# Memory cross-attention of a two-layer decoder: softmax sums from TensorE, the division on the output, and fp16 half products for query and gate

## The chip, the cores and the metric

The kernel runs on one core of one Trainium2 chip. The metric is the device time of one execution in microseconds (us); smaller is better.

## The reference

Input x is 8 batches of 256 tokens by 256 channels, float32. Six layers follow each other, each as x = x + layer(layernorm(x)): attention with 16 heads of 128, a linear attention over a context of 64 tokens, a feed-forward layer with 4-bit weights, an attention over channels, the memory layer, and a feed-forward layer with ternary weights. The change is in the memory layer; cut to what matters it is

```python
x = rmsnorm(hidden_states, norm_w)
q = (x @ wq.T).reshape(B, L, NH, HD)          # NH = 16 heads of HD = 16
k = (memory_tokens @ wk.T).reshape(B, M, NH, HD)   # M = 64
v = (memory_tokens @ wv.T).reshape(B, M, NH, HD)
attn = jnp.einsum('blhd,bmhd->bhlm', q, k) * scale
attn = jnp.where(memory_mask[:, None, None, :], attn, -jnp.inf)
attn = jax.nn.softmax(attn, axis=-1)
attn = jnp.nan_to_num(attn, nan=0.0)
out = jnp.einsum('bhlm,bmhd->blhd', attn, v).reshape(B, L, C)
out = out @ wo.T
gate = jax.nn.sigmoid(x @ wg.T)
return gate * out
```

## The kernel before

The program has two parts. `attention_part` (to 558 us of the span) computes the first attention in 64 steps, 16 heads by 4 pairs of batches, and beside it prepares the weights of later layers at numbered steps: `KV_HI` is step 59, `LAST` is 63. Its scores, exponentials, column sums and products with the rows of X are staged over three steps, so that step i works on step i-1 and i-2 too.

`streams_part` runs the other five layers. A batch is a stream; four streams share the chip at a time, and batches 4 to 7 follow batches 0 to 3 in the same buffers, so there are two rounds, 558 to 735 us and 735 to 912 us. A stream has two PSUM banks, `PA` and `PB`. Each layer of a stream is a list of stages with an engine and a length each (`work`). `turns_by_engine` lays the stages of all streams out in time by these lengths and so fixes the order of each engine's queue; at run time every engine goes through its queue in that order and waits for semaphores. The lengths decide the order only.

A layer starts with its norm: `stats` (L1556), `aggr` (L1562), `eps` (L1568 for the memory layer, L1571 for the others) on VectorE, the power on GpSimd (L1416), the normalised rows, four transposes by TensorE (L1746) and their copy to SBUF by ScalarE. In the memory layer this copy (L1455) also multiplies by `norm_w`. Then TensorE makes queries (`mem_q`, L1731) and gate (`mem_g`, L1738) in float32, four products of 128x128 by 256 columns each. Every tile t of 128 tokens then goes through

- `s`: mask and scores of 16 heads by 64 keys into both banks (PE, L1855 and L1860)
- `max`, `sub` (DVE, L1681, L1684), `exp` (ACT, L1506), `sum`, `rd` (DVE, L1688, L1691: sums of the exponentials of each head, and their reciprocals), `pn` (POOL, L1427: 1024 exponentials times the 16 reciprocals)
- `pt` (PE, L1868: eight transposes), `pte` (ACT, L1510), `o` (PE, L1875: eight products with a 32-column stationary, two heads each, that go to four different groups of 32 output rows in turn), `ote` (ACT, L1516: copy to `ot` times `any_key`)

The tile 1 scores wait for tile 0's `ote`, because they use the same banks. `mem_out` (PE, L1738), `mem_go` and `mem_add` (DVE, L1666, L1670) end the layer. In the ternary layer, `m0`, `c0`, `c1` (L1701 to L1710) make two scalars per row. `pair_matmuls` (L75 to L77) multiplies two float32 operands that are split into fp16 halves, as three fp16 products.

```python
for j in range(XH // 2):
    rows = slice(j % 4 * 2 * XD, (j % 4 + 1) * 2 * XD)
    last = nc.tensor.matmul(PA[s][rows, j // 4 * P:(j // 4 + 1) * P],
                            g.v1[:, s, j].rearrange("p a e -> p (a e)"), pt[s][:, j * P:(j + 1) * P],
                            start=True, stop=True)
```

## Time and profile before

| | before |
|---|---|
| median of 3 runs | 916.41 us (916.15 to 917.59) |
| the profiled execution | 914.14 us, span 912.3 us |
| mean granted TensorE clock | 0.994 |
| TensorE busy | 848.8 us (93%) |
| VectorE busy | 707.6 us (78%) |
| ScalarE busy | 539.0 us (59%) |
| GpSimd busy | 373.0 us (41%) |

The span is the time from the first to the last instruction in the profile; 1.8 us of the execution lie around it. A float32 product shows as two records of TensorE, an fp16 one as one. The length of a record is that of one product in a pipeline, so the cost of a series is read from start to start.

### The profile page before, as it was taken

To read this page: it belongs to the slowest core of one execution; us is meant where nothing else is said; L and a number is where in the kernel's file an instruction comes from. 1 tells how busy PE (TensorE), PEld (TensorE's weight loads), DVE (VectorE), ACT (ScalarE), POOL (GpSimd) and SP (SyncE) were. 2 spreads that over 40 slices of the span, in tenths; PEclk is the share of its full clock that TensorE was granted. 3 is DMA by queue.
4 is the path that set the end of the run, shared out by engine and by line. 5 is a ranking of instruction groups with operands and counts; after the bars stand their busy time and mean duration, and the time that the engine had idled before them with its cause. 6 is when DMAs were issued, how large, how long until landed. Compare 5 with 4: busy or idle time off the path is not lost. (4 is left out here: it accounts for less than half of the span.)

```text
span 912.3 us, 18715 instructions
## 1 busy us (share of the span) xinstructions
PE 848.8 (93%) x6868; PEld 630.7 (69%) x6868; DVE 707.6 (78%) x1749; ACT 539.0 (59%) x1285; POOL 373.0 (41%) x358
## 2 busy tenths in 40 slices
PE   6888998999999999999999998999978889999786
PEld 3555766777777777777777776887855578777554
DVE  5647967887788788877887774997688779886985
ACT  1655576665666566656665655464566864546676
POOL 6014555545555555545554644052242031522410
PEclk9999999999999999999999999999999999999999
DMA  9133131101110111011100000000000010000001
GB/s 279 40 83 93 22 94 36 31 6 35 35 26 8 35 35 35 0 35 35 35 0 11 1 1 2 2 1 1 1 1 1 1 47 1 1 1 1 1 1 47
DMA packets 34723, 25.56 MB, mean 28 GB/s; under 512 B 9492, under 2 KB 31596, under 8 KB 34668
## 3 DMA queue, kind: packets, MB, share of 16 engines
q1 hardware_dynamic: 34380, 24.56, 10.1%
q8 instruction: 35, 0.57, 0.3%
q10 hardware_dynamic: 288, 0.26, 0.1%
q14 instruction: 20, 0.16, 0.1%
HBM read 22.65 MB, written 2.17 MB: 27 GB/s over the span
## 5 line engine op out<-in xcount | busy, mean ns | idle before, releaser
L502 POOL CAST exp_hi<-exp_scores 128x1024 f16<-128x1024 f32 x64 | 67.0, 1047 | 199.4 <-ACT exp_scores L628 199.4
L504 POOL TENSOR_TENSOR exp_lo<-exp_scores,exp_hi 128x1024 f16<-128x1024 f32 x64 | 140.7, 2198 | 5.1
L628 ACT ACTIVATE exp_scores<-banks,exp_bias,unscale 128x256 f32<-128x256 f32 x256 | 141.0, 560 | 2.1
L75 PE MATMUL banks<-value_out_hi,xn_t_hi 128*128 128x256 f16 x512 | 139.6, 273 | 0.8 <-DVE X L961 0.5
L76 PE MATMUL banks<-value_out_lo,xn_t_hi 128*128 128x256 f16 x512 | 139.5, 273 | 0.0
L77 PE MATMUL banks<-value_out_hi,xn_t_lo 128*128 128x256 f16 x512 | 139.5, 273 | 0.0
L1119 PE MATMUL banks<-qk 128*128 128x256 f32 x512 | 121.6, 380 | 8.5 <-ACT exp_scores L628 8.4
L1119 PEld LDWEIGHTS banks<-qk 128*128 128x128 f32 x512 | 96.6, 190 | 29.4 <-issue 8.7
L961 DVE SCALAR_TENSOR_TENSOR X<-banks,colsum,X 128x256 f32<-128x256 f32 x256 | 106.2, 478 | 12.8 <-DVE colsum L952 11.4
L573 ACT ACTIVATE qk<-banks 128x512 f32<-128x512 f32 x128 | 75.8, 601 | 58.9 <-PE banks L77 58.9
L75 PE MATMUL banks<-xn_t_hi,head_weights_hi 128*128 128x512 f16 x256 | 96.9, 378 | 2.4 <-ACT qk L573 1.6
L933 DVE TENSOR_REDUCE neg_rowmax<-banks 128x4 f32<-128x1024 f32 x64 | 78.2, 1222 | 26.7 <-PE banks L1119 26.6
L77 PE MATMUL banks<-xn_t_hi,head_weights_lo 128*128 128x512 f16 x256 | 97.0, 379 | 0.0
L76 PE MATMUL banks<-xn_t_lo,head_weights_hi 128*128 128x512 f16 x256 | 96.9, 379 | 0.0
L1416 POOL TENSOR_TENSOR rstd_stream<-rstd_stream,neg_half 128x2 f32<-128x2 f32 x36 | 26.0, 724 | 137.4 <-DVE rstd_stream L1571 127.2
L624 ACT ACTIVATE exp_bias<-neg_rowmax,unscale 128x4 f32<-128x4 f32 x64 | 18.8, 293 | 99.8 <-DVE neg_rowmax L933 99.8
L76 PEld LDWEIGHTS banks<-value_out_lo,xn_t_hi 128*128 128x128 f16 x512 | 50.1, 98 | 11.8
L442 POOL TENSOR_TENSOR head_weights_lo<-head_weights,head_weights_hi 128x512 f16<-128x512 f32 x32 | 38.8, 1213 | 47.5 <-ACT head_weights_hi L526 47.4
L75 PEld LDWEIGHTS banks<-value_out_hi,xn_t_hi 128*128 128x128 f16 x512 | 50.1, 98 | 10.0 <-DVE X L961 3.4
L1427 POOL TENSOR_TENSOR big_stream<-big_stream,den_stream 128x1024 f32<-128x1024 f32 x16 | 30.3, 1901 | 60.9 <-DVE den_stream L1691 60.9
L77 PEld LDWEIGHTS banks<-value_out_hi,xn_t_lo 128*128 128x128 f16 x512 | 50.1, 98 | 5.8
L628 ACT ACTIVATION_READ_ACCUMULATOR exp_scores<-banks,exp_bias,unscale 128x1 f32 x256 | 50.8, 198 | 0.0
(254 smaller groups left out, 1962.4 us busy)
## 6 DMA issues: line engine op xcount, KB each, us to landing
head_weights<-in_wqkv_d SPq DMA_DIRECT2D x32, 128.0 KB, 3.8
weight_absmax_rows<-across_partitions SPq DMA_DIRECT2D x15, 256.0 KB, 4.2
X<-in_x_d SPq DMA_DIRECT2D x4, 512.0 KB, 7.6
head_weights<-in_wqkvt_d SPq DMA_DIRECT2D x16, 128.0 KB, 3.5
head_weights<-in_w_o_d SPq DMA_DIRECT2D x16, 128.0 KB, 3.5
out<-X SPq DMA_DIRECT2D x8, 256.0 KB, 2.1
ternary_then_kv_and_rows<-in_c_fc_d SPq DMA_DIRECT2D x1, 1024.0 KB, 5.0
ternary_then_kv_and_rows<-in_c_proj_d SPq DMA_DIRECT2D x1, 1024.0 KB, 8.0
```

The lines of the kernel that those rows point to most:

```text
L75: nc.tensor.matmul(out, lhs[0], rhs[0], start=first, stop=False)
L76: nc.tensor.matmul(out, lhs[0], rhs[1], start=False, stop=False)
L77: return nc.tensor.matmul(out, lhs[1], rhs[0], start=False, stop=last)
L442: nc.gpsimd.tensor_tensor(wlo[:, u, 2 * a:2 * a + 2], wst[:, u, 2 * a:2 * a + 2], whi[:, u, 2 * a:2 * a + 2], ALU.subtract).then_inc(wlo_r ...
L502: nc.gpsimd.tensor_copy(probh[:, s1_.par], prob[:, s1_.par]).then_inc(exph_ready, 1)
L504: nc.gpsimd.tensor_tensor(probl[:, s1_.par], prob[:, s1_.par], probh[:, s1_.par], ALU.subtract).then_inc(expl_ready, 1)
L573: nc.scalar.activation(qk[:, par, s, :], qk_ps[s], ACT.Copy).then_inc(qk_ready, 1)
L628: last = nc.scalar.activation(prob[:, s1_.par, t, :], sc_ps[t // ST][:, t % ST, :], ACT.Exp, bias=nbias[:, t:t + 1], scale=unscale[:, s1_. ...
L933: nc.vector.tensor_reduce(nmax[:, :], sc_both, AX.X, ALU.max, negate=True).then_inc(nmax_ready, 1)
L961: last = nc.vector.scalar_tensor_tensor(out=g.X[:, TP * s2.p + t, :], in0=xm_ps[t // ST][:, t % ST, :], scalar=csum[:, t:t + 1], in1=g.X[: ...
L1119: last = nc.tensor.matmul(sc_ps[b][:, t, :], qk[:, par, 0, q], qk[:, par, 1, kk], start=True, stop=True)
L1427: nc.gpsimd.tensor_tensor(by_head(s), by_head(s), den[s][:, t, :].unsqueeze(2).broadcast_to([P, XH, M]), ALU.mult).then_inc(mem_pn[t], 1)
```

## The change

In the attention part, the weights of query and gate are prepared once: multiplied by `norm_w` and their absolute maxima taken (step 59), the maxima spread over the partitions by two DMAs on the SP queue, behind the last head's, and scaled (step 61), and split into fp16 halves (step 62: ScalarE the high, VectorE the low one). GpSimd sets a tile `own_ones`: for each of a pair of heads ones in its 64 rows and 16 columns.

In the memory layer, the transposed rows are split into halves (ScalarE copies the high half, VectorE subtracts for the low one: a new `lo`), and query and gate become 12 fp16 products each. `sum`, `rd`, `pn` and `ote` are gone: the transposes take the exponentials as they are. `o` gets a second product for each pair of heads, with `own_ones`, that leaves the sum of each head in the 16 rows of its output. `rs` takes the reciprocal of these 128x256 sums from PSUM into `xt`, `on` multiplies output, `any_key` and reciprocal into `ot`; both are on VectorE.

In all layers of the streams `eps` moves from VectorE to GpSimd, and in the ternary layer `c1` is folded into `m0` and `c0`. The planner's lengths follow (`rs` .42, `on` .42, `o` 1.16). The two buffers of rows for maxima move into `nf4_part0` and `nf4_part1`.

```diff
+        sp.wait_ge(mem_max_ready, 2)
+        sp.dma_start(spread(6, P, 2), mem_max[:, :]).then_inc(mem_max_out, 16)
+        sp.wait_ge(mem_max_out, 16)
+        sp.dma_start(mem_rows.rearrange("p q s -> p (q s)"), gathered(6, P, 2)).then_inc(mem_max_in, 16)
...
+        nc.gpsimd.memset(g.own_ones[:, :, :], 0.0).then_inc(own_ones_set, 1)
+        for a in range(2):
+            pool.wait_ge(own_ones_set, a + 1)
+            nc.gpsimd.memset(g.own_ones[a * M:(a + 1) * M, a, :], 1.0).then_inc(own_ones_set, 1)
+        pool.wait_ge(own_ones_set, 3)
...
+            if known(i) and i == KV_HI + 3:
+                act.wait_ge(mem_step, 5)
+                for n, (w, (hi, _)) in enumerate(zip(mem_weights, mem_parts)):
+                    nc.scalar.activation(hi, w, ACT.Copy, scale=mem_scale[:, n:n + 1]).then_inc(mem_hi_ready, 1)
...
+            if i == KV_HI:
+
+                dve.wait_ge(late_loads, 16 * len(g.small_loads))
+                for w in (g.wq1, g.wg1):
+                    for k in range(KT):
+                        nc.vector.tensor_scalar(w[:, k, :], w[:, k, :], g.normw[:, k:k + 1], None,
+                                                ALU.mult).then_inc(mem_normed, 1)
+                for n, w in enumerate(mem_weights):
+                    dve.wait_ge(mem_normed, KT * (n + 1))
+                    nc.vector.tensor_reduce(mem_max[:, n:n + 1], w, AX.X, ALU.max,
+                                            apply_absolute_value=True).then_inc(mem_max_ready, 1)
...
+            if i == KV_HI + 2:
+                dve.wait_ge(mem_max_in, 16)
+                nc.vector.tensor_reduce(mem_all[:, :], mem_rows.rearrange("p q s -> p s q"), AX.X,
+                                        ALU.max).then_inc(mem_step, 1)
...
+            if i == KV_HI + 3:
+                dve.wait_ge(mem_hi_ready, 2)
+                for n, (w, (hi, lo)) in enumerate(zip(mem_weights, mem_parts)):
+                    nc.vector.scalar_tensor_tensor(out=lo, in0=w, scalar=mem_scale[:, n:n + 1], in1=hi, op0=ALU.mult,
+                                                   op1=ALU.subtract)
...
-        return [f"{layer}_stats DVE .66 {after}", f"{layer}_aggr DVE .16", f"{layer}_eps DVE .08", f"{layer}_pow POOL .67",
+        return [f"{layer}_stats DVE .66 {after}", f"{layer}_aggr DVE .24", f"{layer}_eps POOL .2", f"{layer}_pow POOL .67",
...
-    work += norm_work("mem", "fat_add", ["xt ACT .74"])
-    work += ["mem_q PE 1.8", "mem_kbd DVE .67 fat_add", "mem_g PE 1.74 mem_xt", "mem_qt ACT .49 mem_q", "mem_ge ACT .49 mem_g"]
+    work += norm_work("mem", "fat_add", ["xt ACT .49", "lo DVE .6"])
+    work += ["mem_q PE 1.36", "mem_kbd DVE .67 fat_add", "mem_g PE 1.36 mem_lo", "mem_qt ACT .49 mem_q", "mem_ge ACT .49 mem_g"]
     for t in range(ST):
         work += [f"mem{t}_{w}" for w in ("s PE 1.19" + (" mem_qt mem_kbd mem_ge" if t == 0 else ""),
-                                         "max DVE 1.13", "sub DVE 1.14", "exp ACT .96", "sum DVE 1.13", "rd DVE .17",
-                                         "pn POOL 1.86", "pt PE 1.02", "pte ACT .92", "o PE .58", "ote ACT .36")]
+                                         "max DVE 1.13", "sub DVE 1.14", "exp ACT .96", "pt PE 1.02", "pte ACT .92",
+                                         "o PE 1.16", "rs DVE .42", "on DVE .42")]
...
+            if part == "eps":
+                ln = norms[layer]
+                pool.wait_ge(ln["mv"], nth_norm(layer, s))
+                inside, eps = (1.0 + 1e-6, LN_EPS * 1e-6) if layer == "mem" else (1.0, LN_EPS)
+                nc.gpsimd.tensor_scalar(rstd[s][:, :], mv[s][:, :, 1], inside, eps, ALU.mult, ALU.add).then_inc(ln["veps"], 1)
...
-            elif part == "pn":
-                t = tile_of(layer)
-                pool.wait_ge(mem_rden[t], n[s])
-                nc.gpsimd.tensor_tensor(by_head(s), by_head(s), den[s][:, t, :].unsqueeze(2).broadcast_to([P, XH, M]),
-                                        ALU.mult).then_inc(mem_pn[t], 1)
...
-                elif layer == "mem":
-                    for k in range(KT):
-                        last = nc.scalar.activation(xt[s][:, k, :], tiles(PA[s])[:, k, :], ACT.Copy,
-                                                    scale=g.normw[:, k:k + 1])
-                    last.then_inc(mem["xt_ready"], 1)
                 else:
-                    nc.scalar.activation(xh[s], tiles(PA[s]), ACT.Copy).then_inc(ffn_hi if layer == "ffn" else ter_hi, 1)
+                    nc.scalar.activation(xh[s], tiles(PA[s]), ACT.Copy).then_inc(xt_hi[layer], 1)
...
-                nc.scalar.activation(qt[s][:, :, :], tiles(PB[s]), ACT.Copy).then_inc(mem_q, 1)
+                nc.scalar.activation(qt[s][:, :, :], tiles(PB[s]), ACT.Copy, scale=g.mem_unscale[:, 0:1]).then_inc(mem_q, 1)
             elif name == "mem_ge":
                 act.wait_ge(mem_g_full, n[s])
-                nc.scalar.activation(gate[s][:, :, :], tiles(PA[s]), ACT.Tanh, scale=0.5).then_inc(mem_g, 1)
+                nc.scalar.activation(gate[s][:, :, :], tiles(PA[s]), ACT.Tanh, scale=g.mem_half_unscale[:, :]).then_inc(mem_g, 1)
...
-            elif layer in ("mem0", "mem1") and part == "ote":
-
-                t = tile_of(layer)
-                act.wait_ge(mem_o_full[t], n[s])
-                nc.scalar.activation(ot[s][:, :, t * P:(t + 1) * P], PA[s][:, 0:KT * P].rearrange("p (k n) -> p k n", k=KT),
-                                     ACT.Copy, scale=g.anykey[:, s:s + 1]).then_inc(mem_o[t], 1)
...
-            elif part == "lo" and layer in ("ffn", "ter"):
-                dve.wait_ge(ffn_hi if layer == "ffn" else ter_hi, n[s])
+            elif part == "lo":
+                dve.wait_ge(xt_hi[layer], n[s])
...
-            elif part == "sum":
-                dve.wait_ge(mem_exp[t], n[s])
-                nc.vector.tensor_reduce(den[s][:, t, :], by_head(s), AX.X, ALU.add).then_inc(mem_sum[t], 1)
-            elif part == "rd":
-                dve.wait_ge(mem_sum[t], n[s])
-                nc.vector.reciprocal(den[s][:, t, :], den[s][:, t, :]).then_inc(mem_rden[t], 1)
+            elif part == "rs":
+                dve.wait_ge(mem_o_full[t], n[s])
+                nc.vector.reciprocal(xt[s][:, t, :], PA[s][:, KT * P:2 * KT * P]).then_inc(mem_rden[t], 1)
+            elif part == "on":
+                dve.wait_ge(mem_rden[t], n[s])
+                by_tile = lambda ap: ap.rearrange("p (k n) -> p k n", k=KT)
+                nc.vector.scalar_tensor_tensor(out=ot[s][:, :, t * P:(t + 1) * P], in0=by_tile(PA[s][:, 0:KT * P]),
+                                               scalar=g.anykey[:, s:s + 1], in1=by_tile(xt[s][:, t, :]), op0=ALU.mult,
+                                               op1=ALU.mult).then_inc(mem_o[t], 1)
...
-                nc.vector.tensor_scalar(small[s][:, 5:6], small[s][:, 4:5], g.tscale[:, 0:1], float(np.sqrt(1e-5)),
-                                        ALU.mult, ALU.max).then_inc(ter_step[s], 1)
+                nc.vector.tensor_scalar(small[s][:, 5:6], small[s][:, 4:5], g.tscale_root[:, 0:1],
+                                        float(np.sqrt(1e-5 / 255.0)), ALU.mult, ALU.max).then_inc(ter_step[s], 1)
             elif part == "c0":
-                dve.wait_ge(ter_step[s], s // STREAMS * 3 * ST + 3 * t + 1)
-                nc.vector.reciprocal(small[s][:, 6:7], small[s][:, 5:6]).then_inc(ter_step[s], 1)
+                dve.wait_ge(ter_step[s], s // STREAMS * 2 * ST + 2 * t + 1)
+                nc.vector.reciprocal(small[s][:, 7:8], small[s][:, 5:6]).then_inc(ter_scale[t], 1)
                 nc.vector.tensor_scalar(small[s][:, 9 + t:10 + t], small[s][:, 5:6], small[s][:, 5:6],
-                                        g.tscale255[:, 0:1], ALU.mult, ALU.mult).then_inc(ter_step[s], 1)
-            elif part == "c1":
-                dve.wait_ge(ter_step[s], s // STREAMS * 3 * ST + 3 * t + 2)
-                nc.vector.tensor_scalar(small[s][:, 7:8], small[s][:, 6:7], float(np.sqrt(255.0)), None,
-                                        ALU.mult).then_inc(ter_scale[t], 1)
...
-                features_first(PB[s], g.wq1, xt[s]).then_inc(mem_q_full, 1)
+                for m in range(KT):
+                    for k in range(KT):
+                        last = pair_matmuls(nc, tiles(PB[s])[:, m, :],
+                                            [w[:, k, m * P:(m + 1) * P] for w in g.mem_halves[0]],
+                                            [x[:, k, :] for x in (xh[s], xl[s])], k == 0, k == KT - 1)
+                last.then_inc(mem_q_full, 1)
             elif name == "mem_g":
-                tokens_first(PA[s], xt[s], g.wg1).then_inc(mem_g_full, 1)
+                for t in range(ST):
+                    for k in range(KT):
+                        last = pair_matmuls(nc, tiles(PA[s])[:, t, :],
+                                            [x[:, k, t * P:(t + 1) * P] for x in (xh[s], xl[s])],
+                                            [w[:, k, :] for w in g.mem_halves[1]], k == 0, k == KT - 1)
+                last.then_inc(mem_g_full, 1)
...
-                pe.wait_ge(mem_pn[t], n[s])
+                pe.wait_ge(mem_exp[t], n[s])
...
-                    last = nc.tensor.matmul(PA[s][rows, j // 4 * P:(j // 4 + 1) * P],
-                                            g.v1[:, s, j].rearrange("p a e -> p (a e)"), pt[s][:, j * P:(j + 1) * P],
-                                            start=True, stop=True)
+                    for at, values in ((j // 4, g.v1[:, s, j]), (KT + j // 4, g.own_ones[:, :, :])):
+                        last = nc.tensor.matmul(PA[s][rows, at * P:(at + 1) * P], values.rearrange("p a e -> p (a e)"),
+                                                pt[s][:, j * P:(j + 1) * P], start=True, stop=True)
...
```

The planner's order changes in the memory layer. TensorE, round one: the products that stand ahead of the first scores. Numbers behind names are the streams; L1818 is the channel attention's first product of stream 3, L1731 and L1738 with `wq1` and `wg1` are query and gate, L1855 and L1860 the scores. Before:

```order
L1818 MATMUL banks<-xn_stream_3 128x256 x4
L1731 MATMUL banks<-xt_stream_0,wq1 128x256 x4
L1738 MATMUL banks<-wg1,xt_stream_0 128x256 x4
L1746 MATMUL banks<-ident,xn_stream_1 128x128 x4
L1826 MATMUL banks<-ident,big_stream_3 128x128 x4
L1746 MATMUL banks<-ident,xn_stream_2 128x128 x4
L1855 MATMUL banks<-mask_bias,ones 128x512 x2
L1860 MATMUL banks<-big_stream_0,qt_stream_0 128x256 x4
```

After the change (the query of stream 0, a turn, the gate of stream 0, two turns, the query of stream 1 and the channel attention's last product of stream 3 stand ahead of these rows; L75 to L77 are half products, L1893 and L1898 the scores):

```order
L75 MATMUL banks<-mem_w1_hi,xt_stream_1 128x256
L76 MATMUL banks<-mem_w1_lo,xt_stream_1 128x256
L77 MATMUL banks<-mem_w1_hi,xt_stream_1 128x256
L1893 MATMUL banks<-mask_bias,ones 128x512 x2
L1898 MATMUL banks<-big_stream_0,qt_stream_0 128x256 x4
L75 MATMUL banks<-xt_stream_2,mem_w0_hi 128x256
L76 MATMUL banks<-xt_stream_2,mem_w0_hi 128x256
L77 MATMUL banks<-xt_stream_2,mem_w0_lo 128x256
L75 MATMUL banks<-xt_stream_2,mem_w0_hi 128x256
```

The first scores of stream 0 have moved behind query and gate of stream 1.

VectorE, round one, inside the layer (before: L1681 max, L1684 sub, L1688 sum, L1691 rd):

```order
L1684 TENSOR_TENSOR big_stream_3<-banks,den_stream_3 128x1024
L1681 TENSOR_REDUCE den_stream_0<-banks 128x16
L1688 TENSOR_REDUCE den_stream_3<-big_stream_3 128x16
L1684 TENSOR_TENSOR big_stream_0<-banks,den_stream_0 128x1024
L1691 RECIPROCAL den_stream_3<-den_stream_3 128x16
L1681 TENSOR_REDUCE den_stream_1<-banks 128x16
L1688 TENSOR_REDUCE den_stream_0<-big_stream_0 128x16
L1684 TENSOR_TENSOR big_stream_1<-banks,den_stream_1 128x1024
L1681 TENSOR_REDUCE den_stream_2<-banks 128x16
```

After (L1710 max, L1713 sub, L1717 rs, L1721 on):

```order
L1710 TENSOR_REDUCE den_stream_3<-banks 128x16
L1717 RECIPROCAL xt_stream_0<-banks 128x256
L1713 TENSOR_TENSOR big_stream_3<-banks,den_stream_3 128x1024
L1721 SCALAR_TENSOR_TENSOR ot_stream_0<-banks,any_key,xt_stream_0 128x2x128
L1717 RECIPROCAL xt_stream_1<-banks 128x256
L1721 SCALAR_TENSOR_TENSOR ot_stream_1<-banks,any_key,xt_stream_1 128x2x128
L1717 RECIPROCAL xt_stream_2<-banks 128x256
L1721 SCALAR_TENSOR_TENSOR ot_stream_2<-banks,any_key,xt_stream_2 128x2x128
L1710 TENSOR_REDUCE den_stream_0<-banks 128x16
L1713 TENSOR_TENSOR big_stream_0<-banks,den_stream_0 128x1024
```

Where sum and reciprocal of a tile stood between maxima, there is now a reciprocal of 256 elements a row and the multiplication, later in the stream's tile, and the second tiles' maxima come behind three of them.

## Rows read from the trace of the kernel before

**Rows 1.** Windows of the first round: start:end, length, then busy us (instructions) per engine.

```profile
596.50:643.10 46.60, 46.35 (x342) 37.23 (x341) 38.91 (x111) 25.00 (x69) 19.68 (x30) 1.00 0.01 1
643.10:649.10 6.00, 6.00 (x40) 4.96 (x39) 2.42 (x10) 4.98 (x13) 0.70 (x1) 1.00 0.00 0
649.10:659.10 10.00, 10.00 (x51) 8.28 (x52) 6.11 (x13) 4.46 (x8) 2.56 (x2) 1.00 0.00 1
659.10:684.30 25.20, 20.62 (x192) 14.89 (x196) 21.73 (x25) 14.80 (x19) 9.93 (x6) 0.93 0.01 1
684.30:700.10 15.80, 14.69 (x134) 11.37 (x127) 13.76 (x32) 8.95 (x14) 5.43 (x5) 1.00 0.01 2
700.10:734.80 34.70, 27.20 (x203) 16.90 (x201) 27.73 (x83) 28.01 (x31) 3.78 (x5) 1.00 0.07 23
```

**Rows 2.** Timeline of TensorE, first round: start us, length us, group xrecords.

```profile
641.22 1.89 PE L1818 MATMUL banks<-xn_stream 128*128 128x256 f32 x8
642.94 1.89 PE L1731 MATMUL banks<-xt_stream,wq 128*128 128x256 f32 x8
...
648.03 1.03 PE L1860 MATMUL banks<-big_stream,qt_stream 64*128 64x256 f32 x8
648.99 1.99 PE L1738 MATMUL banks<-big_stream,xt_stream 128*128 128x256 f32 x8
...
667.13 0.65 PE L1875 MATMUL banks<-mid_stream,v 128*32 128x128 f32 x16 [0.58 <-ACT mid_stream L1510]
667.71 1.09 PE L1868 MATMUL banks<-ident,big_stream 128*128 128x128 f32 x8
```

**Rows 3.** Timeline of VectorE: first row maximum and last gated addition of round one.

```profile
649.11 1.23 DVE L1681 TENSOR_REDUCE den_stream<-banks 128x16 f32<-128x1024 f32 x1 [2.62 <-PE banks L1860]
...
699.36 0.69 DVE L1670 SCALAR_TENSOR_TENSOR X<-gate_stream,X 128x512 f32<-128x512 f32 x1
```

**Rows 4.** Groups by line and shape, VectorE reciprocals: xcount | busy us, mean ns.

```profile
L1691 DVE RECIPROCAL den_stream<-den_stream 128x16 f32<-128x16 f32 x16 | 3.6, 237 | 0.0
...
L1609 DVE RECIPROCAL den_stream<-den_stream 128x32 f32<-128x32 f32 x8 | 2.8, 351 | 0.1
...
L793 DVE RECIPROCAL nf_divide<-nf_s_by_column 128x66 f32<-128x66 bf16 x1 | 0.6, 567 | 0.1
```

**Rows 5.** Groups by line and shape, other VectorE and ScalarE work of the layers.

```profile
L1688 DVE TENSOR_REDUCE den_stream<-big_stream 128x16 f32<-128x1024 f32 x16 | 19.4, 1212 | 1.9 <-ACT big_stream L1506 1.9
...
L1585 DVE TENSOR_TENSOR xt_stream<-banks,xt_stream 128x512 f16<-128x512 f32 x16 | 10.9, 678 | 0.0
...
L1571 DVE TENSOR_SCALAR rstd_stream<-mv_stream 128x2 f32<-128x2 f32 x28 | 7.7, 273 | 0.4
...
L1516 ACT ACTIVATE ot_stream<-banks,any_key 128x256 f32<-128x256 f32 x16 | 7.5, 468 | 7.1 <-PE banks L1875 7.1
...
L1613 DVE SCALAR_TENSOR_TENSOR xn_stream<-banks,lin_scale,den_stream 128x256 f32<-128x256 f32 x16 | 7.0, 478 | 0.2
```

**Rows 6.** Timeline of VectorE inside the memory layer.

```profile
671.18 1.21 DVE L1688 TENSOR_REDUCE den_stream<-big_stream 128x16 f32<-128x1024 f32 x1
672.31 1.22 DVE L1684 TENSOR_TENSOR big_stream<-banks,den_stream 128x1024 f32<-128x1024 f32 x1
```

**Rows 7.** Groups by line and shape, GpSimd.

```profile
L1427 POOL TENSOR_TENSOR big_stream<-big_stream,den_stream 128x1024 f32<-128x1024 f32 x16 | 30.3, 1901 | 60.9 <-DVE den_stream L1691 60.9
...
L507 POOL TENSOR_TENSOR rowsum_inverse_halves<-rowsum_inverse,rowsum_inverse_halves 128x4 f16<-128x4 f32 x64 | 13.7, 215 | 6.5 <-DVE rowsum_inverse_halves L918 6.5
```

**Rows 8.** The chain of waits, first round: four transposes, then 16 fp16 products.

```profile
595.26 0.44 PE banks L1746 x4
595.69 1.75 PE banks L1800 x16
```

**Rows 9.** Timeline of VectorE at the end of the attention part.

```profile
514.30 1.22 DVE L933 TENSOR_REDUCE neg_rowmax<-banks 128x4 f32<-128x1024 f32 x1 [1.96 <-PE banks L1119]
...
541.13 0.22 DVE L949 TENSOR_SCALAR colsum_raw<-banks,unscale 128x4 f32<-128x4 f32 x1 [0.48 <-PE banks L1199]
```

More of the change, by code:

```diff
@@ L2040, in decoder @@
     g.normw = table("normw", KT)
+    g.mem_halves = [[sb(f"mem_w{n}_{half}", [P, KT, D], F16) for half in ("hi", "lo")] for n in range(2)]
+    g.mem_unscale = sb("mem_w_unscale", [P, 2])
+    g.mem_half_unscale = sb("mem_w_half_unscale", [P, 1])
     g.headmask = table("headmask", XH // KT)
```

62 lines of the change are left out of this document (36 added, 26 removed).

## Prediction

> **What bounds the kernel now.** I read the windows of the first round first, since the streams run twice with the same order and almost the same length. In the feed-forward and channel attention stretch TensorE is busy 46.35 of 46.60 us, and it stays full while the memory layer starts, 643.1 to 659.1 us; VectorE is busy there 2.42 of 6 and 6.11 of 10 us. Then it turns over: from 659.1 to 700.1 us VectorE is busy 35.5 of 41.0 us and TensorE waits 5.7 us. In the ternary stretch no engine is full; TensorE, VectorE and ScalarE are each near 80% [rows 1]. So the change is worth something in two places with two different limits: what it takes off TensorE's queue before the first scores, and what it puts on or takes off VectorE between the first row maximum at 649.1 and the last gated addition at 700.05 us (699.36 + 0.69), a stretch of 51.0 us [rows 3].
>
> **Query and gate.** A float32 product of one kind takes from the start of the series at 641.22 to the next at 642.94, 1.73 us for four products [rows 2]. Sixteen fp16 products of the same 256 columns take 1.75 us, 0.109 each [rows 8], so twelve take 1.31: 0.42 saved, for each of two products of a stream, 3.4 us of TensorE a round. But the order changes as well. Before, query, gate, three sets of four transposes and the scores stand between the end of the last channel product, 643.1, and the first scores' end, 649.1. In the new order query and gate of stream 1 and the last channel product stand there too: four series at 1.31, three sets of transposes at 0.44 [rows 8], one float32 series at 1.92 (start 648.99, seen from its end) and the scores with mask at 1.2, 9.7 us; I add 0.3 for `lo`, which the query now waits for. VectorE has room for it. The first scores end 4.0 us later than before, and what was done in that time needn't be done afterwards.
>
> **The stretch from there.** VectorE is busy 6.11 + 21.73 + 13.76 = 41.6 us in the 51.0 [rows 1]. Eight tiles have a maximum, a subtraction and a sum each, at 1.13 from start to start [rows 6] for a length of 1.21 [rows 5]: lengths overlap by 0.08. With eight small reciprocals at 0.237 - 0.08 = 0.16 [rows 4] these are 28.4 us; 13.2 us are other work.
>
> - Gone: `sum` and `rd`, 8 x (1.13 + 0.16) = 10.3 us.
> - New: `on`, 8 x 0.40 by the like multiplication of 128x256 from PSUM, 0.478 long [rows 5], 3.2 us.
> - New: `rs`. No row shows a reciprocal of 256 elements. 16, 32 and 66 elements take 237, 351 and 567 ns [rows 4]: 7.1 and 6.4 ns for each further one, where the multiplication of 256 takes 478 in all. The lower bound is that 478 ns, if the slope came from something else than the operation; the upper is 0.351 + 224 x 0.0071 = 1.94 us. I take the slope of the widest row: 0.567 + 190 x 0.0064 = 1.78, less the overlap 1.70, 8 x 1.70 = 13.6 us. The order that the planner made counts on 0.42.
> - The other work: the last channel addition, its statistics and means fall before the new first scores (1.6 us less), four `eps` go to GpSimd (4 x 0.273, 1.1 less) [rows 5], the last stream's `lo` comes in (0.6 more, L1585's 0.678 less the overlap) [rows 5]: 11.1 us.
>
> The maxima and subtractions stay, 18.1. Sum 18.1 + 13.6 + 3.2 + 11.1 = 46.0 us. VectorE waits at two places: the second maximum is behind query and gate of stream 2 and the scores (1.4 us), the fourth behind those of stream 3 (1.2). That makes 48.6 for 51.0. With the later start: +4.0 - 2.4 = **+1.6 us a round**.
>
> The Trainium skill, VectorE: DVE Perf Modes (First, the fixed hardware budget), says that a reciprocal is an iterative divide with a repeat count of 8. At the clock that its Specifications give, 0.96 GHz, my estimate from that page is 8.3 ns an element and 2.1 us for 256; `rs` would add 3 us a round to the sum above. The rows, at 6.4 to 7.1 ns, have the same kind of cost but a smaller one, and the sum goes by them.
>
> **`o` doubled.** Eight products and their 16 records show 0.65 us [rows 2]. The bounds for sixteen: 0.65, if the second of a pair fits in the shadow of the first, and 2.0, if it doesn't overlap at all with a product before it on the same output rows: a float32 product of 256 columns is 0.43 (1.73 / 4), of 128 columns 0.22, eight pairs that follow at that pace make 1.73 and the last result 0.28. I take 1.2, twice the row. TensorE then has about 42.6 us of work in the 48.6: 45.3 before [rows 1], 5.4 that moved ahead, 1.7 off the later queries and gates, 4.4 more in `o`. So it is hidden behind VectorE, as long as it stays near 1.2.
>
> **The chain of a tile.** `sum`, `rd`, `pn` (1.90 us on GpSimd [rows 7]) and `ote` (0.47 on ScalarE [rows 5]) were 3.7 us from exponential to transposes and from output to the next scores; `rs` and `on` are 2.1. That helps only where VectorE waits, and it is in the two waits that I left.
>
> **Rest of a round.** Eight `c1` at 0.07 and the `eps` of the other layers in full VectorE stretches at 0.08 are worth 1.2 us. The `eps` on GpSimd costs 0.2 (by L507, 0.215 [rows 7]) against less on VectorE, and a norm's rows wait for it a few times: 0.5 back. **-0.7 us a round.** ScalarE's lighter load is worth nothing: it was waiting.
>
> **Attention part.** Step 59 puts four multiplications and two maxima, about 2.5 us, where VectorE is idle 1.96 us before the next row maximum [rows 9]; TensorE doesn't wait for that maximum yet. The two DMAs have a step and a half, on a queue with nothing behind them but the end. Step 61's 1.5 us fit in idle time. Step 62 adds two subtractions, 1.3 us, just before the first statistics, where VectorE's next wait is only 0.48 us [rows 9]: I take 0.7 for all (0 to 2). The memsets of `own_ones` are under 0.5 us on an idle GpSimd, zero; without that cover the first weights' halves, and the first scores behind them, would be that much later.
>
> **Sum:** 2 x (1.6 - 0.7) + 0.7 = +2.5 us on the span of 912.3 in an execution of 914.14. That execution lies 2.3 us under the median of the runs, 916.41, and I add the difference to the median: **918.9 us**. About 0.2% (1.8 us) is what a measurement tells from no change, so this is just beyond it.
>
> **Rivals.**
> - *Pairs on the same output rows wait for each other.* Before, neighbours in `o` go to different groups of rows, which is how eight products fit in 0.65 us; now each second one follows its own pair. `o` is then 2.0, TensorE's work in the stretch 49.0 us, above VectorE's 46.0, and the first `rs` starts 0.8 later. I price it at +2 us a round: 922.9. For it: the pace of one after another, 1.73, is far above the 0.65 seen. The Trainium skill, TensorEngine Tiling (Array Packing), Key Properties, says that different tiles work in parallel; no trace here has two products in a row on the same one. Chance 0.24.
> - *The reciprocal runs like other operations at this width* (faster side). The rows stop at 66 elements. At 0.48 instead of 1.78, `rs` takes 10.4 us a round off VectorE, and TensorE's 42.6 us plus a wait bound the stretch: -5 a round, 908.9. It decides from about 1.2 us down; at 1.5 the change is nil. Against it: three widths on one line. Chance 0.12.
> - *Waits vanish more than I count* (the shorter tile chain, and VectorE's `eps` that had stood still for GpSimd, 0.273 against 0.16 for an undisturbed one): -3 a round, 912.9. Chance 0.14.
> - *The order fits lengths that aren't true.* `rs` is planned at a quarter of its length, so maxima queue behind reciprocals whose sums aren't there, and ScalarE and TensorE wait in turn: +3 a round, 924.9. Chance 0.14.
> - That the change doesn't do what it says I leave out: the order shows every stage in its new place.
>
> **How the numbers follow.** The forecast has 0.36. Its own spread of some 3 us puts a quarter of it within 0.2%, and a little below. The range from 911 to 925 leaves out most of the fast reciprocal and half of the misfit, under 0.2. Faster by over 0.2% (under 914.6): 0.12, most of 0.14 and a little of the forecast, 0.26. Within: 0.22, from the forecast and the edges of its neighbours. Slower: 0.52.
>
> **What would show it.** The first row maximum some 4 us later in the round, the gated additions ending 1 to 2 us later; `rs` at 1.7 to 1.8 us, and VectorE the releaser of TensorE's waits in the layer; `o` at 1.2 us from start to start; query and gate at 1.3 each; no `pn` on GpSimd; 0 to 2 us more before the streams start. A `rs` under 1.2 us, or VectorE idle over 5 us in the layer while TensorE is full, would prove the forecast wrong.

## The result, and the profile after

The changed kernel takes **924.85 us** (median of 5 runs, 923.42 to 927.95), the kernel before 916.41: 1.0092 times as long, 95% interval 1.0069 to 1.0116. The forecast was 918.9. The profiled execution has a span of 923.1 us against 912.3, and that of before lay 2.3 us under its own median, so the traces show 10.8 us where the medians show 8.4.

The groups that answer to [rows 4, 5, 7, 8], by line and shape (the last two columns: busy us with mean ns, and idle time before with its releasers):

```profile
L1717 DVE RECIPROCAL xt_stream<-banks 128x256 f32<-128x256 f32 x16 | 28.0, 1747 | 0.0
...
L1614 DVE TENSOR_TENSOR xt_stream<-banks,xt_stream 128x512 f16<-128x512 f32 x24 | 16.4, 682 | 2.9 <-ACT xt_stream L1503 2.8
...
L75 PE MATMUL banks<-xt_stream,mem_w_hi 128*128 128x256 f16 x32 | 8.8, 274 | 0.2
...
L1466 POOL TENSOR_SCALAR rstd_stream<-mv_stream 128x2 f32<-128x2 f32 x36 | 7.8, 216 | 219.3 <-DVE mv_stream L1600 219.0
...
L1721 DVE SCALAR_TENSOR_TENSOR ot_stream<-banks,any_key,xt_stream 128x256 f32<-128x256 f32 x16 | 7.7, 479 | 0.3
```

The new operations last what the prediction said: `rs` 1.75 us (1.78), `on` 0.48, `eps` on GpSimd 0.216. The doubled `o`, on TensorE's timeline (start, length, group xrecords):

```profile
672.04 0.45 PE L1914 MATMUL banks<-mid_stream,v 128*32 128x128 f32 x8
672.28 0.42 PE L1914 MATMUL banks<-mid_stream,own_ones 128*32 128x128 f32 x8
672.50 0.44 PE L1914 MATMUL banks<-mid_stream,v 128*32 128x128 f32 x8
672.72 0.44 PE L1914 MATMUL banks<-mid_stream,own_ones 128*32 128x128 f32 x8
673.09 1.09 PE L1906 MATMUL banks<-ident,big_stream 128*128 128x128 f32 x8
```

Sixteen products in 1.05 us, start to next start. No pair waits for its neighbour on the same output rows.

**Where the time went.** Marks of the two timelines, each piece in us (the pieces tile the span). The next-to-last scores are the 63rd of the attention part's 64; the first stream operation is VectorE's on `headmask`; fat_e is the channel attention's first product, and its last in a round is that of the fourth stream:

| piece | before | after | difference |
|---|---|---|---|
| start to the next-to-last scores | 536.21 | 537.01 | +0.8 |
| from there to the first stream operation | 21.95 | 27.73 | **+5.8** |
| round one: to the last fat_e | 83.06 | 84.29 | +1.2 |
| to the first row maximum | 7.89 | 11.68 | **+3.8** |
| to the fourth gated addition | 50.25 | 47.87 | -2.4 |
| round two: to the last fat_e | 118.54 | 117.62 | -0.9 |
| to the first row maximum | 7.90 | 11.68 | **+3.8** |
| to the fourth gated addition | 48.75 | 47.66 | -1.1 |
| to the end | 37.75 | 37.56 | -0.2 |

The streams together cost 4.2 us, the attention part 5.8, the start 0.8. The fences below mark rows left out between two shown by `...`. The two ends of the big piece in the attention part, on VectorE's and then TensorE's timeline of the changed kernel (in brackets: idle time before, and its releaser):

```profile
537.82 2.71 DVE L1045 SCALAR_TENSOR_TENSOR mem_w_lo<-wq,mem_w_scale,mem_w_hi 128x512 f16<-128x512 f32 x1 [0.99 <-ACT mem_w_hi L662]
540.45 0.74 DVE L1045 SCALAR_TENSOR_TENSOR mem_w_lo<-wg,mem_w_scale,mem_w_hi 128x512 f16<-128x512 f32 x1
...
543.16 1.22 DVE L954 TENSOR_REDUCE neg_rowmax<-banks 128x4 f32<-128x1024 f32 x1
```

```profile
537.01 1.89 PE L1169 MATMUL banks<-qk 128*128 128x256 f32 x8
...
547.18 3.46 PE L1169 MATMUL banks<-qk 128*128 128x256 f32 x8 [3.99 <-ACT exp_scores L645]
```

The same places in the kernel before, the row maximum and the two sets of scores:

```profile
538.13 1.22 DVE L933 TENSOR_REDUCE neg_rowmax<-banks 128x4 f32<-128x1024 f32 x1
```

```profile
536.21 1.89 PE L1119 MATMUL banks<-qk 128*128 128x256 f32 x8
...
542.16 1.97 PE L1119 MATMUL banks<-qk 128*128 128x256 f32 x8
```

VectorE waits 0.99 us for ScalarE's high halves, then needs 2.71 us for one subtraction that takes 0.74 the second time. GpSimd's timeline has the reason beside it, the subtraction that makes the exponentials' low half (exp_lo):

```profile
537.85 2.13 POOL L521 TENSOR_TENSOR exp_lo<-exp_scores,exp_hi 128x1024 f16<-128x1024 f32 x1
```

The long subtraction ends at 540.53, 0.55 us after exp_lo's end at 539.98: it stood still until GpSimd was through. The Trainium skill, GPSIMD Engine Reference (1. Specifications), lists GpSimd's way to SBUF as shared with VectorE, with contention where VectorE has two SBUF inputs, as here. The row maximum behind it comes at 543.16 (538.13 before), the exponentials after it, and TensorE stands for 3.99 us. The granted clock around it:

```profile
540.00:550.00 10.00, 5.84 (x49) 4.58 (x48) 7.85 (x26) 3.89 (x11) 3.93 (x4) 0.84 0.01 2
550.00:560.00 10.00, 9.14 (x93) 7.61 (x92) 8.38 (x22) 4.98 (x13) 4.95 (x6) 0.99 0.00 0
...
564.70:574.70 10.00, 9.96 (x36) 7.58 (x38) 2.55 (x3) 3.44 (x7) 4.93 (x4) 0.70 0.01 2
```

These are windows: bounds, length, busy us of TensorE, its weight loads, VectorE, ScalarE and GpSimd, and the granted clock. In a window with a mean of 0.84 or 0.70, part of the time is at 1.2 GHz and the rest at 2.4. After the 3.99 us of standing, the scores at 547.18 take 3.46 us for what took 1.97. The last window is the beginning of the streams, where TensorE has stood 3.16 us. In the kernel before it had stood 3.10 us, and their first 10 us have a clock of 0.85:

```profile
558.20:568.20 10.00, 10.00 (x44) 7.54 (x45) 2.60 (x4) 4.85 (x10) 4.88 (x4) 0.85 0.01 2
```

The first piece of round one takes 1.2 us more, and over the kernels below clock and length go together: 0.70 to 0.73 in the first 10 us of the streams with 84.0 to 84.4 us for the piece (changed, lo_end, length_17, halves_only, lo_end_l17), 0.83 to 0.85 with 83.0 to 83.2 us (the other eight, without replanned, whose order there is another). All five kernels without prepared weights are in the second group, but old_streams, copy_for_reciprocal and lo_last are too; whether the preparation makes the low clock likelier stays open.

The 0.8 us at the start are no work of the change. TensorE's clock was low for longer there, in the windows 38 to 42, 42 to 44 and 44 to 46 us (clock 0.53, 0.50 and 0.74; before 0.63, 0.89 and 1.00). In the traces of the other kernels below, whose queues are nearly the same up to that point, the next-to-last scores come at 535.9 to 543.1 us. So I compare the last two columns of the table below, which leave this part out.

### The profile page after: what moved, and what is told of

Same layout as the page of the kernel before. It is cut to its first block and busy times, and to the rows that moved or that the text cites. A ratio compares the mean times of both kernels' runs of the same rounds, so it can differ in the third digit from the quotient of the medians.

```text
span 923.1 us, 19329 instructions
## 1 busy us (share of the span) xinstructions
PE 858.6 (93%) x7188; PEld 638.0 (69%) x7188; DVE 727.4 (79%) x1719; ACT 533.1 (58%) x1263; POOL 350.0 (38%) x381
## 5 line engine op out<-in xcount | busy, mean ns | idle before, releaser
L521 POOL TENSOR_TENSOR exp_lo<-exp_scores,exp_hi 128x1024 f16<-128x1024 f32 x64 | 138.6, 2165 | 5.1
L75 PE MATMUL banks<-value_out_hi,xn_t_hi 128*128 128x256 f16 x512 | 139.6, 273 | 0.8 <-DVE X L982 0.6
L77 PE MATMUL banks<-value_out_hi,xn_t_lo 128*128 128x256 f16 x512 | 139.6, 273 | 0.0
L75 PE MATMUL banks<-xn_t_hi,head_weights_hi 128*128 128x512 f16 x256 | 97.6, 381 | 2.4 <-ACT qk L590 1.6
L77 PE MATMUL banks<-xn_t_hi,head_weights_lo 128*128 128x512 f16 x256 | 97.7, 382 | 0.0
L1466 POOL TENSOR_SCALAR rstd_stream<-mv_stream 128x2 f32<-128x2 f32 x36 | 7.8, 216 | 219.3 <-DVE mv_stream L1600 219.0
L75 PEld LDWEIGHTS banks<-value_out_hi,xn_t_hi 128*128 128x128 f16 x512 | 50.1, 98 | 10.0 <-DVE X L982 3.5
L77 PEld LDWEIGHTS banks<-value_out_hi,xn_t_lo 128*128 128x128 f16 x512 | 50.1, 98 | 5.8
L540 ACT ACTIVATE head_weights<-head_weights,weight_scale 128x256 f32<-128x256 f32 x64 | 28.9, 502 | 31.1 <-DVE weight_scale L725 31.1
```

Source lines behind the costliest of these rows:

```text
L75: nc.tensor.matmul(out, lhs[0], rhs[0], start=first, stop=False)
L77: return nc.tensor.matmul(out, lhs[1], rhs[0], start=False, stop=last)
L521: nc.gpsimd.tensor_tensor(probl[:, s1_.par], prob[:, s1_.par], probh[:, s1_.par], ALU.subtract).then_inc(expl_ready, 1)
```

## The experiments

All times are medians against the kernel before on the same chip (its median was 916.2 to 916.7 in every set). "Scores" is the start of the next-to-last scores, "to streams" runs from there to the first stream operation, "streams" from there to the end of the span; these three are from one trace of each kernel.

| kernel | us | ratio, 95% | scores | to streams | streams |
|---|---|---|---|---|---|
| before | 916.41 | | 536.2 | 21.95 | 354.1 |
| changed | 924.85 | 1.0092 (1.0069 to 1.0116) | 537.0 | 27.73 | 358.4 |
| old_streams | 921.66 | 1.0054 (1.0037 to 1.0071) | 536.1 | 28.34 | 354.3 |
| lo_last | 922.40 | 1.0069 (1.0044 to 1.0093) | 535.9 | 25.95 | 358.1 |
| lo_end | 921.58 | 1.0056 (1.0037 to 1.0074) | 536.0 | 24.08 | 358.0 |
| copy_for_reciprocal | 911.59 | 0.9949 (0.9927 to 0.9971) | 537.7 | 28.23 | 343.5 |
| length_17 | 922.34 | 1.0061 (1.0038 to 1.0084) | 537.3 | 27.87 | 355.5 |
| halves_only | 927.69 | 1.0113 (1.0080 to 1.0145) | 539.2 | 27.72 | 362.0 |
| fp32_products | 935.88 | 1.0186 (1.0157 to 1.0215) | 541.2 | 22.02 | 371.1 |
| fp32_l17 | 929.85 | 1.0143 (1.0112 to 1.0174) | 538.0 | 22.02 | 367.9 |
| neither | 924.39 | 1.0071 (1.0047 to 1.0096) | 538.5 | 22.01 | 362.4 |
| fp32_same_order | 926.16 | 1.0089 (1.0068 to 1.0111) | 543.1 | 22.01 | 364.8 |
| lo_end_l17 | 919.00 | 1.0018 (1.0005 to 1.0032) | 540.2 | 24.09 | 355.4 |
| replanned | 912.82 | 0.9955 (0.9938 to 0.9973) | 537.5 | 24.08 | 349.5 |

**Streams or attention part? (old_streams)** The streams of before behind the changed attention part. Their weights are already multiplied by `norm_w`, so against the kernel before their code differs in one scale and one renamed tile (the other edits, not shown, are the attention part's):

```diff
-                        scale=g.normw[:, k:k + 1])
+                        scale=1.0)
```

> The changed attention part with the streams of before (weights already multiplied by the norm's, so the scale of that product's copy is 1). Theory (6 to 7 us of the loss lie ahead of the streams): 916.4 + 5 to 7 = 921.5 to 923.5, streams begin at 563 to 565. Rival (the loss is the streams' alone: reciprocal, doubled sums, eps on GpSimd): 916.5 to 918.

Measured 921.66, streams 354.3, to streams 28.34. Shown: the preparation of the weights costs about 6 us there (6.4 in the trace, 5.5 in the median), and nothing downstream takes it back.

**The subtraction one step later (lo_last), and at the end (lo_end).**

```diff
-            if i == KV_HI + 3:
+            if i == KV_HI + 4:
                 dve.wait_ge(mem_hi_ready, 2)
```

> Theory (most of the loss is made at the attention part's end, where VectorE subtracts the high from the whole weights, 0.99 + 2.71 + 0.74 us, ahead of the row maximum of step 62): one step later this work lies in the 2.63 us in which VectorE waited for TensorE, the row maximum comes about 4 us earlier, TensorE's 3.99 us of waiting at 547 and the low clock of 560 to 570 (0.69) go, the streams begin at 560 to 561 instead of 564.7, and the time is 919.5 to 921.5. Rival (the streams take up whatever the attention part loses, the reciprocals set the end): streams earlier, the time still 924 to 925.

> The subtraction of the weights' halves stands behind VectorE's last operation of the attention part, where the kernel before had 1.64 us idle ahead of the streams and GpSimd has nothing. Theory (in the attention part only the subtraction ahead of a row maximum costs: it took 2.71 + 0.74 us beside GpSimd's exp_lo, and one step later, 0.97 + 2.61 us, it cost nearly as much): it takes 0.74 twice, the streams begin at 558.2 to 559.5, and the time is 917.5 to 920 (924.9 - 5 to 6.5). Rival (steps 59 and 61, and ScalarE's high halves in 62, cost as well): streams at 561 or later, 921 to 923.

`lo_last` came out between the two: 1.8 us of 5.8 back. VectorE's timeline shows why the idle time that I had put it into was not there any more:

```profile
543.49 0.97 DVE L1045 SCALAR_TENSOR_TENSOR mem_w_lo<-wq,mem_w_scale,mem_w_hi 128x512 f16<-128x512 f32 x1
544.38 2.61 DVE L1045 SCALAR_TENSOR_TENSOR mem_w_lo<-wg,mem_w_scale,mem_w_hi 128x512 f16<-128x512 f32 x1
...
547.07 1.19 DVE L954 TENSOR_REDUCE neg_rowmax<-banks 128x4 f32<-128x1024 f32 x1
```

The 2.63 us of waiting ahead of the last row maximum were in part a result of the late work before. With that on time 1.13 us of them are left (`lo_end`'s trace), and the next exp_lo (543.99, 2.45 us long) held up the other subtraction. Placed behind VectorE's last operation (the same two statements after the loop) it meets no GpSimd work:

```profile
557.24 0.74 DVE L1079 SCALAR_TENSOR_TENSOR mem_w_lo<-wq,mem_w_scale,mem_w_hi 128x512 f16<-128x512 f32 x1
557.89 0.75 DVE L1079 SCALAR_TENSOR_TENSOR mem_w_lo<-wg,mem_w_scale,mem_w_hi 128x512 f16<-128x512 f32 x1
560.12 1.27 DVE L1580 TENSOR_TENSOR headmask<-headmask 128x4 f32<-128x4 f32 x1 [1.47 <-PEq L2021]
```

3.7 of 5.8 us are back. Of the other 2.1, 1.0 is TensorE's wait ahead of the last scores, for exponentials that stand behind ScalarE's high halves (1.08 us of idle time at 542.96, `<-ACT exp_scores`), and 1.2 is the subtraction itself, behind which VectorE's first stream operation comes later. Both theories of `lo_end` had a part of it: the streams begin at 560.1 us, between the two, but its median fell by less (3.3 us) than the theory wanted (5 to 6.5) and lies in the rival's range.

Steps 59 and 61 cost nothing, though they last longer than forecast (4.0 and 3.2 us on VectorE, since operations there stand still beside exp_lo too). The two steps of TensorE from the fourth-last scores to the next-to-last take 15.15 us in the kernels with prepared weights and 15.84 in those without, and the step ahead of them, in which step 59's work lies, takes 8.0 us in both. The fourth-last scores:

```profile
521.86 1.89 PE L1169 MATMUL banks<-qk 128*128 128x256 f32 x8
```

```profile
520.37 1.89 PE L1119 MATMUL banks<-qk 128*128 128x256 f32 x8
```

The first is the changed kernel, the second the one before. In the latter, step 60's subtraction (L1000) and exp_lo began together at 519.45 us and took 4.89 and 4.31 us; in the changed kernel exp_lo begins later, at 524.29, and they take 3.80 and 2.16.

**What the reciprocals cost (copy_for_reciprocal).** The division by the sums is left out.

```diff
-                nc.vector.reciprocal(xt[s][:, t, :], PA[s][:, KT * P:2 * KT * P])
+                nc.vector.tensor_copy(xt[s][:, t, :], PA[s][:, KT * P:2 * KT * P])
```

> The reciprocal of the sums (1747 ns) becomes a copy of the same tile (division by the sums left out), about 1.3 us less for each of 16. Theory (VectorE sets the memory stretch, 46 of 48.6 us busy): 8 to 10 us less in each round, 924.9 - 16 to 20 = 905 to 909. Rival (the reciprocals lie beside other work): 1 to 2 us a round less, 921 to 923.

The copy takes 417 ns instead of 1747, 21.3 us less in all; the streams get 14.9 us shorter. Of these, 1.3 are the low clock at the streams' beginning, which this trace hasn't got (83.04 us for 84.29), so 13.6, or 64% of the saving, are on the path. The median fell by 13.3 us, less than the theory's 16 to 20 and far more than the rival's 2 to 4. The rest isn't on the path, since TensorE then fills the stretch, 40.44 of 41.70 us busy in round one:

```profile
660.60:702.30 41.70, 40.44 (x488) 31.51 (x487) 35.14 (x59) 22.87 (x28) 2.69 (x6) 1.00 0.01 2
```

**The planner's lengths (length_17).** The planner writes the four queues from a list of lengths, in which `rs` had .42.

```diff
-                                         "o PE 1.16", "rs DVE .42", "on DVE .42")]
+                                         "o PE 1.16", "rs DVE 1.7", "on DVE .42")]
```

> The planner gets 1.7 us instead of .42 as the reciprocal's length; the operations stay. Theory (the order was written for a short reciprocal, but VectorE is busy nearly always, so the order matters little): 923.5 to 925.5. Rival (the order does not fit the lengths): 2 to 4 us less, 921 to 923; slower if the new order spoils the ternary stretch.

2.9 us of the streams and 2.5 of the median, the rival's size. My theory falls: VectorE was busy nearly always in that stretch, and still the order was worth 3 us.

**The four corners (halves_only, fp32_products, neither).** The change has two parts, products of halves and the new softmax. `halves_only` has the first with the softmax of before, `fp32_products` the second with float32 products and no preparation, `neither` has neither: beside the memsets only `eps` on GpSimd and one VectorE operation less in each ternary tile stay, with the planner's entries for them (`aggr` .24 and `eps POOL .2` for `aggr` .16 and `eps DVE .08`, and no `c1` of .08).

> The other half: products of halves and their preparation, but sums, reciprocals of 128x8, GpSimd's product and ScalarE's eviction as before. Theory: 916.4 + 6 (attention part) + 2 x 3.8 (first scores) + 0 to 5 (four more VectorE subtractions a round in its full stretch) - 1.5 = 926 to 933, slower than the whole change. Rival (the halves are harmless, the reciprocals cost): 917 to 921.

> Only the softmax half of the change: q and g are fp32 products with the copy scaled by the norm's weight as before, nothing is prepared in the attention part. Theory (the halves cost the attention part 6 us and delay the first scores by 3.8 us in each round, the new division by itself gains about 1 us a round): streams begin at 558 to 559, last fat_e start to first row maximum 7.9 us instead of 11.7, stretch to the fourth gated add 45 to 48 us, the time 907 to 912. Rival (the reciprocal is what costs, the halves are paid for by TensorE): 917 to 921.

> The fourth corner: products fp32 and softmax divided as before; what is left of the change is eps on GpSimd, one VectorE operation less in each ternary tile, and the planner's lengths for these. Theory (forecast in the prediction as 0.7 us less in each round): streams 352 to 354 us against 354.1, the time 914 to 916.5. Rival (a changed order again costs more than the operations): 918 or more.

Only `halves_only` came out as said; its trace has a clock of 0.87 in round one's memory stretch (53.2 us, 49.9 in round two), so some 3 us of its 362.0 in the streams are low clock. `fp32_products` is the slowest kernel of all, its streams 17 us longer than before, and `neither`, whose operations are almost those of before, takes 8.3 us more in the streams. TensorE's timeline of `neither` between the last product of the fat layer and the first scores:

```profile
643.54 1.89 PE L1823 MATMUL banks<-xn_stream 128*128 128x256 f32 x8
645.27 1.89 PE L1736 MATMUL banks<-xt_stream,wq 128*128 128x256 f32 x8
647.00 1.89 PE L1743 MATMUL banks<-wg,xt_stream 128*128 128x256 f32 x8
648.73 0.60 PE L1831 MATMUL banks<-ident,big_stream 128*128 128x128 f32 x4
649.16 1.04 PE L1751 MATMUL banks<-ident,xn_stream 128*128 128x128 f32 x8
650.07 1.99 PE L1743 MATMUL banks<-big_stream,xt_stream 128*128 128x256 f32 x8
651.90 1.89 PE L1736 MATMUL banks<-xt_stream,wq 128*128 128x256 f32 x8
653.62 1.89 PE L1743 MATMUL banks<-wg,xt_stream 128*128 128x256 f32 x8
655.45 0.39 PE L1860 MATMUL banks<-mask_bias,ones 64*128 64x512 bf16 x2
655.67 1.03 PE L1865 MATMUL banks<-big_stream,qt_stream 64*128 64x256 f32 x8
```

The scores of stream 0 stand behind query and gate of stream 1 and the last channel product, as in the changed kernel; before, they came right after the transposes [rows 2]. No half product is in this kernel. So the late first scores, the 3.8 us twice in the table above, aren't made by the halves: the planner turned the queue round when its list changed by a tenth of a microsecond here and there, in the norms and in the ternary tile.

**The length again, and the order held still (fp32_l17, fp32_same_order).** The first is `fp32_products` with `rs` at 1.7. The second has its float32 operations, but the planner's lengths and so the queues of the changed kernel (VectorE's place for the mem layer's low half stays empty, so those subtractions are gone too).

> The softmax half with the planner's length of the reciprocal set to 1.7 us. Theory: 1 to 3 us less than the softmax half alone (the same edit took 2.5 us off the whole change), 905 to 910. Rival (the order was right for fp32 products): no difference to it.

> The softmax half alone came out at 935.9 us, its streams lasting 371.1 us against 358.4 of the whole change; but its planner lengths were those of fp32 products, so its order differed too. Here the products are fp32 as in that run, the planner's lengths those of the whole change, so each queue has the changed kernel's order (VectorE's slot of the mem layer's low half stays empty). Theory (the order cost the 13 us): streams 356 to 361 us, the time 919 to 922, less than the whole change because nothing is prepared. Rival (fp32 products in the full TensorE stretch cost it): streams 365 to 371, the time 930 to 935.

`fp32_l17` gained the 3 us in the streams again (371.1 to 367.9), though not the level that I had given. `fp32_same_order` came between its two ranges (926.16) and split the difference of 12.7 us in the streams: 6.3 are the order, 6.4 the float32 products. Both figures hold some clock. About 1.6 of the 6.3 may be `fp32_products`' round one, whose memory stretch takes 52.65 us at a clock of 0.91 and 51.05 at 0.97 in round two. And the changed kernel's first piece holds 1.2 us of low clock that `fp32_same_order` hasn't got, so its products cost rather more than 6.4. The products themselves are 16 x (1.73 - 1.31) = 6.7 us of TensorE, so with the order held that work is about all on the path. (ScalarE's copy is longer too, and eight of VectorE's subtractions are gone; no run takes these apart.)

**Both mends, and another order (lo_end_l17, replanned).**

> The whole change with both mends: the subtraction of the weights' halves behind the attention part's last VectorE operation, and 1.7 us as the reciprocal's length. Theory (they are independent: 4.4 us in the attention part, 2.5 to 2.9 in the streams): 917.5 to 919.5, still 1 to 3 above the kernel before. Rival (they share a gain): 920 to 922.

919.0: the two gains add up, and 2.3 us above the kernel before remain. Then, with every operation kept, only the planner's lengths:

```diff
+    planned = {'mem_rs': 1.7, 'ter_n': 0.18, 'mem_add': 0.69, 'ter_add': 0.64, 'ter_sh': 0.16, 'ter_nt': 0.72,
+               'fat_out': 1.56, 'mem_xt': 0.64, 'mem_pte': 0.46, 'mem_ge': 0.15, 'fat_xn': 1.04, 'fat_eps': 0.6,
+               'fat_add': 0.69, 'mem_lo': 0.51, 'fat_pow': 0.87}
...
+        work[i] = " ".join([name, eng, str(planned.get(key, took)), *rest])
     turns = turns_by_engine(work)
```

> All operations of the changed kernel, the subtraction of the weights' halves at the attention part's end, and fifteen of the planner's lengths changed, so that the four queues stand in another order in the fat, mem and ter layers; the order was picked by the end that it gives when each queue is walked with the durations of the traces and 0.2 us between an operation and its user, a walk that gave 352.7, 357.5, 353.4 and 341.7 us for streams that took 354.1, 358.4, 355.5 and 343.5. Theory (the order of the queues, not what the new operations last, keeps the change from paying): streams 347 to 350 us instead of 355.4, the time 911 to 914, faster than both kernels. Rival (the operations' own work fills VectorE, no order helps): 355 us and 918 to 920.

**912.82 us**, 3.6 below the kernel before and 12.0 below the change as it was written: streams 349.5 us. The fifteen lengths were picked for the order that they give, not as truer ones. Both rounds have the same stretch from the first row maximum to the fourth gated addition:

```profile
655.40:702.80 47.40, 40.71 (x492) 31.40 (x491) 44.93 (x64) 23.67 (x29) 3.35 (x6) 1.00 0.01 2
828.30:875.70 47.40, 40.72 (x492) 31.38 (x491) 44.93 (x64) 23.67 (x29) 3.36 (x6) 1.00 0.01 1
```

VectorE is busy 44.93 of 47.40 us, as in the changed kernel (45.16 of 48.60), so the stretch gains only 1.2 us in round one and 1.0 in round two. The largest part of the 8.8 us is gained between the rounds: from the fourth gated addition to the last fat_e of round two it is 113.8 us, against 117.6. The first piece of round one gives 2.9 (81.4), the end of round two 1.4. The first scores are even later than before this mend (12.4 us for 11.7), and it doesn't hurt. What stays open: no such order was tried for the operations of before, which may gain as much, so this run doesn't show that the new operations beat the old ones at their best, only that they beat the kernel before.

## Why the prediction was right or wrong

The sign was right. That the range, 911 to 925, held the time is luck: 924.85 lies 0.15 us under its end, two of the five executions lie above it, and the sum was +2.5 us for a measured +8.4. The sum had +0.7 for the attention part and +1.8 for the streams; the traces show +5.8 and +4.2. Point by point:

- **`rs`, `on`, `eps`, query and gate:** right to a few hundredths. 1.75 us for the 1.78 drawn from the slope of three narrower rows. My estimate of 2.1 us from the Trainium skill, VectorE: DVE Perf Modes (First, the fixed hardware budget), was too high; the measurement decides, 1747 ns for 256 elements.
- **First scores 4.0 us later:** right in size, 3.8 in both rounds. It was counted from the order, and the order was indeed the cause; `neither`, which has it without any half product, shows that it wasn't theirs, as I had booked it under "Query and gate".
- **The stretch, 48.6 for 51.0:** 48.53 in round one (660.71 to the end of the addition at 709.24), so the count of VectorE's work and waits held. What failed is its other side: 51.0 was a stretch with a low clock, 0.93 from 659.1 to 684.3 [rows 1]. Round two of the same trace takes 49.4 for the same work (825.80 to 875.24). In `old_streams`, which has the same streams, it is the other way round: up to the start of the fourth addition 48.67 us at a clock of 1.00 in round one and 50.25 at 0.97 in round two (before: 50.25 and 48.75). The changed kernel's stretch doesn't feel it: 47.87 and 47.66 us at 0.96, and 47.87 and 47.67 at 1.00 in `lo_last`. The gain was 2.4 in one round and 1.1 in the other, where the sum had 2.4 twice.
- **`o` at 1.2, pairs don't wait:** 1.05. The rival of the waiting pairs falls, with the pace of one product after another on the same rows, 1.73, that had spoken for it. The Trainium skill, TensorEngine Tiling (Array Packing), Key Properties, promises independence only to different tiles; on the same tile, too, the trace shows no loss.
- **Rest of a round, -0.7:** -0.9 and -0.2 in round two and its end, none in round one, and there 1.2 us of low clock on top. In `lo_last` the same first piece takes 83.04 us, as before; the 1.2 are no work of the streams, and the sum didn't have them.
- **Attention part, 0.7 (0 to 2): the term that failed,** at +5.8. I priced step 62's two subtractions at 1.3 us by what such an operation lasts alone; they took 3.3, behind 0.99 of waiting. The trace of before had GpSimd's exp_lo at that very time, 535.96 to 538.08, and both of its inputs and those of the subtraction are in SBUF; I looked at VectorE's idle time only. The wait for ScalarE's high halves (0.99 us) and the scores behind ScalarE (1.0 us) were not in the sum, nor that TensorE's idle time is paid a second time in clock (3.46 us for 1.97). Steps 59 and 61 were right at nothing, but their lengths were not: 4.0 us for 2.5 and 3.2 for 1.5.
- **The order doesn't fit the lengths (0.14, 924.9):** this rival was right in its mechanism, 2.9 us by `length_17`, and its time came out nearly exact for another reason, since most of the loss was elsewhere. It should have had more weight and a wider price: up to 6.3 us between the orders of `fp32_products` and `fp32_same_order`, 8.3 in `neither`, 5.9 between `lo_end_l17` and `replanned`, whose operations are the same.
- **The fast reciprocal (0.12):** fell with the first row. By `copy_for_reciprocal` its price would have been 13.6 us or 6.8 a round, where I had 5.
- **Waits vanish (0.14):** they didn't. VectorE waited for the second and the fourth maximum, 1.43 and 1.44 us, where 1.4 and 1.2 were forecast.

## What to carry to other kernels

Where a planner or a scheduler orders the queues, a changed length is a change of its own: hold the order still to price an operation, and search the order before judging the change. An operation put "into idle time" ahead of something that others wait for must be priced with what the neighbouring engines do at that moment, and idle time that is itself the result of a delay isn't there once the delay is mended. A stretch taken as the baseline should be read in a second round or its granted clock looked at first, and clocks of two traces compared in windows that begin at the same operation.

## What the runs showed of the hardware

- VectorE's subtraction with two SBUF inputs stood still beside GpSimd's exp_lo: 2.71 and 2.61 us, 0.74 alone, and both times it ended 0.55 us after exp_lo. The Trainium skill, Trainium Architecture — The Big Picture (What this means for kernel authors), says of the ports that VectorE and GpSimd share that they are an exclusive lock and not a split of bandwidth; the trace agrees.
- It isn't only operations with two SBUF inputs, and it goes both ways. In step 61 a `tensor_scalar` of 128x2 took 2.09 us beside exp_lo, its neighbour of 128x1 alone 0.14:

```profile
530.43 2.09 DVE L1037 TENSOR_SCALAR mem_w_unscale<-mem_w_max_all 128x2 f32<-128x2 f32 x1
532.43 0.14 DVE L1038 TENSOR_SCALAR mem_w_half_unscale<-mem_w_max_all 128x1 f32<-128x1 f32 x1
```

  And in the kernel before exp_lo itself took 4.31 us at 519.46, beside VectorE's subtraction of step 60, for 2.13 elsewhere.
- VectorE's reciprocal from PSUM costs 1747 ns for 256 elements, a copy of the same tile 417.
- After standing 3.99 us TensorE took 3.46 us for scores that took 1.97 before, in a window with a granted clock of 0.84. Where the streams begin it has stood 3.1 to 4.3 us in every kernel, and their first 10 us then have a clock of 0.70 to 0.73 or of 0.83 to 0.85; why it differs stays open.
- The same startup reaches the next-to-last scores at 535.9 to 543.1 us in different traces. Part of it is how long TensorE's clock stays low between 38 and 46 us; for the largest values the cause stays open.
